# Masked attention layer: a pair's two normalising products issued by Pool, after a signal from VectorE

## The reference

```python
qh, kh, vh = (proj(q, Wq, bq), proj(k, Wk, bk), proj(v, Wv, bv))
scores = jnp.einsum('bhqd,bhkd->bhqk', qh, kh) / jnp.sqrt(jnp.float32(D_K))
scores = jnp.where(mask[:, None] == 0, jnp.float32(-1000000000.0), scores)
attn = jax.nn.softmax(scores, axis=-1)
ctx = jnp.einsum('bhqk,bhkd->bhqd', attn, vh)
concat = ctx.transpose(0, 2, 1, 3).reshape(bs, -1, INPUT_DIM)
return concat @ Wo.T + bo
```

## Time and profile before

| | |
|---|---|
| median of 3 runs | 4500.99 us (4493.58, 4500.99, 4504.22) |
| the profiled execution | 4493.35 us, its span 4491.5 us |
| PE busy in the span | 4094.5 us (91%) |
| DVE | 2557.7 us (57%) |
| ACT | 1704.6 us (38%) |
| Pool | 1800.2 us (40%) |

### The profile page before, as it was taken

The page is one execution under the profiler, slowest core; times in us unless marked ns, Lnnn a source line. Parts: engine busy times, 40 slices in busy tenths (PEclk is TensorE's granted clock), DMA queues, the critical chain, the costliest instruction groups (busy, mean ns, idle before and its releaser), DMA issues. The chain is left out here.

```text
span 4491.5 us, 65447 instructions
## 1 busy us (share of the span) xinstructions
PE 4094.5 (91%) x20596; PEld 2374.2 (53%) x20596; DVE 2557.7 (57%) x4092; ACT 1704.6 (38%) x3114; POOL 1800.2 (40%) x1263
## 2 busy tenths in 40 slices
PE   4899989989999999899989988998998599999998
PEld 3543744364446436443644364436443477777776
DVE  2564456446534655576567566756674555565554
ACT  1355145425443553344234424442444322222222
POOL 2223122222241224476357535754664244444343
PEclk8999999999998999999999999999999799999998
DMA  2321232132213224322422333223220300000000
GB/s 82 73 50 48 71 93 59 53 85 65 56 51 94 52 62 150 85 43 72 141 67 43 90 127 76 53 94 119 57 43 20 139 27 27 27 29 30 29 29 12
DMA packets 136375, 294.68 MB, mean 66 GB/s; under 512 B 19856, under 2 KB 37904, under 8 KB 136016
## 3 DMA queue, kind: packets, MB, share of 16 engines
q1 hardware_dynamic: 125520, 272.93, 22.5%
q10 hardware_dynamic: 10496, 17.31, 1.1%
HBM read 145.74 MB, written 43.25 MB: 42 GB/s over the span
## 5 line engine op out<-in xcount | busy, mean ns | idle before, releaser
L1133 ACT ACTIVATE probs_a<-half_a 128x512 f32<-128x512 f32 x2048 | 1120.8, 595 | 976.7 <-PE half_a L934 451.0
L931 PE MATMUL half_a<-stack_a 97*128 97x512 f32 x2048 | 874.0, 485 | 75.1 <-DMA stack_a<-mrow_a 36.5
L1369 DVE TENSOR_REDUCE mx_a<-wide_a 128x1 f32<-128x1024 f32 x512 | 601.3, 1219 | 548.3 <-PE wide_a L890 542.3
L1365 DVE CUSTOM_DVE_ANT_0 wide_a<-wide_a,mask_q_a 128x1024 f32<-128x1024 f32 x512 | 619.5, 1245 | 289.3 <-PE wide_a L890 278.4
L890 PE MATMUL wide_a<-stack_a 96*128 96x512 f32 x2048 | 674.3, 438 | 61.3 <-DVE mx_a L1369 31.0
L931 PEld LDWEIGHTS half_a<-stack_a 97*128 97x128 f32 x2048 | 377.3, 194 | 633.1 <-ACT probs_a L1133 326.3
L779 POOL TENSOR_TENSOR psums_a<-psums_a,probs_a 128x1024 f32<-128x1024 f32 x232 | 559.7, 2432 | 144.2 <-ACT probs_a L1133 121.3
L1758 PE MATMUL work_e<-w_in_e,x_e 128*128 128x512 f32 x2304 | 573.9, 401 | 17.7 <-DVEq L2014 10.3
L873 PE MATMUL acc_a<-probs_a,v_a 128*32 128x512 f32 x4096 | 553.0, 610 | 3.1 <-ACT u_a L1104 3.0
L890 PEld LDWEIGHTS wide_a<-stack_a 96*128 96x128 f32 x2048 | 386.0, 196 | 230.7 <-DVE mx_a L1369 57.0
L1758 PEld LDWEIGHTS work_e<-w_in_e,x_e 128*128 128x128 f32 x2304 | 429.7, 191 | 119.4 <-issue 20.3
(11 more groups left out here) (238 smaller groups left out, 4558.9 us busy)
## 6 DMA issues: line engine op xcount, KB each, us to landing
stack_a<-qk_a SPq DMA_DIRECT2D x336, 256.0 KB, 4.9
y_a<-x SPq DMA_DIRECT2D x8, 2048.0 KB, 8.8
x<-y_a SPq DMA_DIRECT2D x8, 2048.0 KB, 7.5
mstage_a<-mask SPq DMA_DIRECT2D x32, 512.0 KB, 4.3
mstage_a<-mask_t SPq DMA_DIRECT2D x32, 512.0 KB, 4.1
stage_a<-x_t SPq DMA_DIRECT2D x24, 512.0 KB, 3.7
stack_a<-first_a SPq DMA_DIRECT2D x48, 256.0 KB, 5.0
x_t<-xts_late_a ACTq DMA_DIRECT2D x10, 1024.0 KB, 7.6
```

Of the source, the lines that this page charges most:

```text
L931: last = pe.matmul(bank[:, :], stack[0:3 * DH + 1, s, 2 + h, kt * P:(kt + 1) * P], stack[0:3 * DH + 1, s, h, c * CH:(c + 1) * CH], start=T ...
L1133: act.activation(probs[:, kt % 2 * 2 + h, c * CH:(c + 1) * CH], bank[:, :], ACT.Exp, scale=SCALE).then_inc(free, 1)
L1365: dve.tensor_tensor_reduce(bank[:, :], bank[:, :], mask_q[:, t, :], 1.0, -3e38, ALU.add, ALU.max, mx[:, p % 3, n:n + 1]).then_inc(free, 1)
L1369: dve.tensor_reduce(mx[:, p % 3, n:n + 1], bank[:, :], AX.X, ALU.max).then_inc(free, 1)
```

## The change

Parts 5 and 6 of `norm` in the masked layer are issued by Pool and no longer by DVE, with the same operands. DVE signals a new semaphore `sums_over` after the last reciprocal; Pool waits for it ahead of part 5. `normed` and `ctx_done` are now signalled by Pool. The list of steps is unchanged, so Pool does the products where the list has them.

```diff
@@ Pool
+                    elif kind == "norm" and sec.att == 1 and step[2] >= 5:
+                        _, p, part = step
+                        c = part - 5
+                        a = 2 * DH * (p % 2)
+                        rows_ = slice(2 * DH * c, 2 * DH * (c + 1))
+                        if c == 0:
+                            pool.wait_ge(sums_over, masked_norms.upto(sec, ("norm", p, 0)))
+                            alone(pool)
+                        pool.tensor_tensor(q_raw[a:a + 2 * DH, p // 2, c * CH:(c + 1) * CH], u[rows_, 0, :],
+                                           u[rows_, 1, :], ALU.mult)
+                        pool.drain()
+                        if p == PAIRS - 1:
+                            pool.engine_nop().then_inc(ctx_done, 1)
+                        if c == 1:
+                            pool.engine_nop().then_inc(normed, 1)
@@ DVE
                             dve.reciprocal(some, some)
-                            dve.drain()
-                        else:
-                            c = part - 5
-                            a = 2 * DH * (p % 2)
-                            rows_ = slice(2 * DH * c, 2 * DH * (c + 1))
-                            last = dve.tensor_tensor(q_raw[a:a + 2 * DH, p // 2, c * CH:(c + 1) * CH], u[rows_, 0, :],
-                                                     u[rows_, 1, :], ALU.mult)
-                            if c == 1:
-                                last.then_inc(normed, 1)
-                            if p == PAIRS - 1:
-                                dve.drain().then_inc(ctx_done, 1)
+                            last = dve.drain()
+                            if part == 4:
+                                last.then_inc(sums_over, 1)
```

More of the change, by code:

```diff
@@ L466, in attention @@
         sums_taken = sem("sums_taken")
+        sums_over = sem("sums_over")
         added = sem("added")
```

## The result

The changed kernel takes **4566.9 us** (median of 4 runs, 4561.07 to 4574.61); the kernel before, run beside it, takes 4499.18 us. The ratio is 1.0155, 95% interval 1.0141 to 1.0168: slower by 1.6%, 67.7 us by the medians. The forecast was 4551 with a range of 4524 to 4574, so direction and range held, and the point was 14 us (by the differences) to 16 us (by the times) short. The profiled execution took 4571.61 us (span 4569.8), 78.3 us more than the profiled one of before (4493.35).

A forecast was written before the change was run, and what follows sets the result against it. Pool's adds from kt = 4 on were taken to bound a pair, through ACT's wait. Terms 13.4 + 6.7 + 31.7 + 1.8 = 53.6 us, put on 4497.3, gave 4551 us, range 4524 to 4574.

The forecast's parts named there:

- The pair's circle through Pool: Masked layer's pairs: Pool's adds from kt = 4 on release ACT's first exponential and so set a pair's length.
- the relief: Pairs 1 to 4: DVE's products no longer delay two Pool adds, giving back 0.84 us a pair.
- the net price of pairs 1 to 4: Product and gap between adds cost 1.68 us, less 0.84 relief: 0.84 us a pair, 13.4 us for 16.
- Pair 6: Same 1.68 us between adds, without relief: 6.7 us over four batches, bounds 6 to 8.
- Pair 5: Cost 0: Pool's later last add still ends before PE's wait for the `mrow` DMA lets ACT start.
- "The 15 us idle get no term": Changed tail: PE's longer idle time before the output products brings no longer slow-clock stretch, so no cost.
- the rival of 19 us a tail: Clock rival: PE stays at its lower level through the other output matmuls, 19 us more a tail, 4608; chance 0.04.
- The tails: Three tails of section 3: `bo` adds queue behind pair 7's products, delaying PE 10.6 us each, 31.7 in all.
- ACT's earlier `ct`: In the tails ACT's `ct` is released by the first product, but PE still waits for Pool's part behind `bo`.
- "Nothing later has slack for it": Behind the tails, output products, layer norm and next K and Q follow on each other, so the delay stays whole.
- The last tail: Section 4, no `bo` ahead: products on Pool make `ct` 0 1.8 us later.
- Port and price of the product: Product takes 1.27 us on Pool against 690 ns on DVE; the full lock rule would return 1.38 us a pair.

The follow-up runs named there:

- the kernel without the products: Kernel before with the two products of pairs 0 to 6 left out, signals kept: 4488.74 us, ratio 0.9996.
- mended kernel: Changed kernel with part 5's product moved to tile 6 behind the add and `bo` ahead of the V tiles: 4499.66 us, ratio 1.0006.
- kernel with `bo` first: Changed kernel with a tail's eight `bo` adds placed ahead of the V tiles: 4542.26 us, ratio 1.0111.
- the one with the product twice: Products of pairs 0 to 6 on Pool, pair 7's on DVE, part 5's product issued twice: 4581.61 us, profiled once, no ratio.
- the one with a quarter: Pairs 0 to 6 on Pool, pair 7 on DVE, only 128 of part 5's 512 columns between the adds: 4496.66 us, ratio 1.0005.
- best version: Pairs 0 to 6 on Pool with both products behind the last add, pair 7's on DVE: 4483.14 us, ratio 0.9975 to the kernel before.
- mended kernel with moved splits: All products on Pool, part 5 at tile 6, `bo` first, `wk` splits moved to output tiles 3 and 4: 4497.76 us, ratio 1.0004.

## Why the prediction was right, and what it missed

- **The pair's circle through Pool: right.** ACT's first exponential starts 0.07 us behind Pool's last add before and 0.08 after; the relief is 0.84 us forecast and 0.75 to 0.83 in the kernel without the products; the net price of pairs 1 to 4 is 0.84 us forecast, and by pair 0.80, 1.03, 0.81 and 0.73 where the clock stays at 1.00 (38.43, 37.85, 38.17 and 37.62 us, from the batches that kept it). PE's shorter wait ahead of `mneg` shows nowhere in it.
- **Pair 6: right in its own term.** 1.68 us forecast; pair 6 of the last batch, at a clock of 1.00, grew by 1.50 (34.92 to 36.42). In the other three batches it grew by 3.1, and the four together by 10.9 us, outside the 6 to 8 us that the bounds gave it.
- **Pair 5: right.** 40.59 us against 40.55 in the first batch, at the same clock.
- **"The 15 us idle get no term": right where it was said, and the step that failed.** In the tail the granted clock reads 0.56 in the stretch to 2206 and 1.00 behind it, so the level of 1.2 GHz ends 5.9 us behind the restart at 2199.84, against 5.4 in the trace before (2174.51 to about 2180); the rival of 19 us a tail is refuted. But the prediction looked for the clock in the tail alone. In the pairs the sum had no term for it, and there it costs 1.55 to 1.71 us in each of 8 pairs (five of pairs 1 to 4, three of pair 6), beyond the 0.73 to 1.03 and the 1.50 of the pairs that kept it: some 13.1 us. Forecast and measured pairs, 20.1 and 29.2, differ by 9.1 only, because pair 5 got 2.5 us of clock back, the last batch's pairs 1 to 4 grew by 0.58 to 0.66 (0.9 less than the forecast in sum), and pair 6 by 1.50 for 1.68 (0.7 less). That pair 5 gave some of it back was luck. The range held although it had no room for this term: its bounds for the product's price and for the relief were not needed, and covered it. Longer and shorter waits of PE changed how often the clock falls, from none of 60 pairs at up to 1.69 us to 16 of 20 at 2.55 us and more. That shows the wait as the cause in the pairs of the kernels run; which single pair is hit it doesn't tell.
- **The tails: right.** Of 10.6 us each 9.9, 10.4 and 10.3 came (sum 30.6 against 31.7). Moving `bo` alone left 1.8 us of them. ACT's earlier `ct` paid nothing, as forecast.
- **"Nothing later has slack for it": incomplete.** The output products follow at once, but the new time at which they start puts DVE's first two-operand instruction on Pool's split: +2.3 and +2.4 us in two of three tails. The moved splits showed this in the mended kernel: the tail that stayed long is the one in which DVE loses 2.0 us to two more of them.
- **The last tail: right**, 1.46 us for 1.8. Two numbers beside the sum are loose: by the prediction's own times `bo` would start at 2173.0, not near 2172, and 84 of 96 products at its pace are 19.7 us.
- **Port and price of the product.** The 1.85 times of the earlier trace rows held (1275 to 690 ns). The rule of the Trainium skill (SBUF — State Buffer, "SBUF: two separate sides") was an exclusive lock for a whole instruction. By it, 1.38 us would come back in a pair; the traces don't agree: 0.75 to 0.83 came back with the products gone altogether. For the instruction on the losing side it fits better: DVE's 2.96 us next to a split of 2.40 us is 2.2 us more than its 0.75. That instruction is the one stretched although its row starts 0.02 us ahead of the split's.

**Open.** From K product to the next batch's copy a kernel takes 120 to 128 us, before too, and the three sum to 373.0 us before, 378.0 changed, 382.4 in the kernel with `bo` first, 379.0 in the one with the product twice and 368.0 in the one with a quarter. The last two have pair 7's products on DVE and no changed instruction in that stretch, so its length is not tied to the change by these traces. It goes with two waits of PE that differ from batch to batch: 1.98 or 4.15 us for DVE ahead of L898 (L914 after), and 3.3 to 6.3 us for the small DMA from `mrow`. The granted clock of the stretch goes with them, 0.96 over the shortest one before (122.06 us) and 0.93 over the longest one after (128.31 us). One execution of each kernel was profiled, and so the several us by which a profiled execution lies off its median are not assigned. It is also open why a pair with the same idle time of PE loses its clock in one batch and keeps it in another (pair 1: 1.53 us idle and 40.00 us long, 1.55 us idle and 38.43 long), and why all 64 products on Pool end no better than the kernel before although their pairs are as short as in the best version. By stretches, the profiled execution of the mended kernel with moved splits wins 11.9 us in the pairs and gives back 2.1 from V to output, 1.6 from output to K, 1.9 from K to the next copy and 4.6 behind the last copy. That last stretch takes 1040.8 to 1044.7 us in all five kernels with pair 7's products on Pool, and 1034.2 to 1037.5 in seven of the eight others; the eighth, with the products left out, takes 1042.1, so this too is not tied to the change.

## What to carry to other kernels

Work that goes to a slower engine should stand where that engine is idle, and not at the first place where its operands are ready: the same products cost 0.7% between two adds and win 0.25% behind the last one. Ahead of a new wait on an in-order engine, read what is queued behind it; eight adds that had been done in the shadow of the V tiles were some 30 us of this loss, and ahead of the wait 1.8 us of that were left. When an edit lengthens a wait of PE, even by 1.5 us, look at the granted clock in stretches of 2 us right behind that wait, and compare every place that waits longer, not only the longest one.

## What the hardware showed unexpectedly

- The granted clock fell after idle times of PE of 1.5 to 2.5 us within a busy pair, in some batches and not in others, and the fall cost about as much as one product on Pool (1.3 to 1.7 us a fall); after 14.68 us idle in the tail the slow stretch was 5.9 us, after 4.33 us it was 5.4.
- A DVE instruction with two operands that starts together with a Pool split of 128x1024 takes 2.96 us instead of 0.75; the split itself takes 2.40 us here, what it takes elsewhere (2.38). Together with a Pool `ct` part of 128x512 (1.29 us) it takes 1.88.
